# Local layers of a macaron block: order of the slot work on SyncE, TensorE and VectorE, banks of the recurrent norms, and another way to make two bias offsets

## The reference, cut to what matters

```python
x = x + 0.5 * _L0_ffn_ref(_layernorm(x), ...)      # token-mixing feed-forward
x = x + _L0_attn_ref(_layernorm(x), ...)           # 16 heads of 64, full attention with a relative bias
x = x + 0.5 * _L0_ffn_ref(_layernorm(x), ...)
x = x + 0.5 * _L1_ffn_ref(x, ...)                  # two "local" layers
x = x + _L1_attn_ref(x, ...)                       # gated recurrence over the 512 tokens
x = x + 0.5 * _L1_ffn_ref(x, ...)                  # the same two local layers again
```

```python
h = shift_token(x)                      # the second half of the features comes from the token before
q, k, v = split(h @ wqkv)               # 8 heads of 64; q and k normalised, scaled, rotated
x = x + local_attention(q, k, v) @ wo   # windows of 64 tokens, each sees itself and the one before
h = (shift_token(x) - mean) / sqrt(var + 1e-5) * lg + lb
a, g = split(h @ w1 + b1)               # 341 columns each, padded to 384
x = x + (a * gelu(g)) @ w2 + b2
```

## Time and profile before

| what | value |
|---|---|
| three runs | 1172.5, 1173.42, 1178.5 us, median 1173.42 |
| the profiled execution, its own time | 1176.82 us |
| its span, first to last instruction | 1175.0 us |
| TensorE busy | 1133.3 us, 96% of the span |
| VectorE, ScalarE, GpSimd busy | 913.7, 920.0, 617.8 us |
| mean granted TensorE clock | 0.993 of full speed |

### The profile page before, as it was taken

How to read it: one execution, slowest core, us unless ns; L and a number is a source line. 1 busy time by engine, 2 the same in 40 slices (tenths; PEclk the granted TensorE clock), 3 DMA queues, 4 the chain that set the end, 5 groups by cost and what they waited for, 6 DMA issues and landing times.

```text
span 1175.0 us, 40447 instructions
## 1 busy us (share of the span) xinstructions
PE 1133.3 (96%) x16054; PEld 728.5 (62%) x16054; DVE 913.7 (78%) x2423; ACT 920.0 (78%) x2451; POOL 617.8 (53%) x406
## 2 busy tenths in 40 slices
PE   8899999999999998999999999988999899999997
PEld 3367777677777653666666666554556566666664
DVE  5788989898989878877777777757787777777763
ACT  6877878787878777887787787876778778978874
POOL 4456666666666644664555455433454554644540
PEclk9999999999999999999999999999999999999999
DMA  8411111111111123111111111011010111111110
GB/s 291 149 39 40 58 40 57 40 57 40 57 39 57 40 85 102 42 33 42 28 42 42 22 39 33 19 33 37 15 41 20 41 32 29 44 40 28 33 42 19
DMA packets 30364, 58.36 MB, mean 50 GB/s; under 512 B 5680, under 2 KB 7152, under 8 KB 30176
## 3 DMA queue, kind: packets, MB, share of 16 engines
q1 hardware_dynamic: 30176, 55.77, 17.4%
HBM read 15.32 MB, written 1.11 MB: 14 GB/s over the span
## 4 chain that ended last, share of the span: by engine, by line
PE 83%; ACT 8%; issue 3%; DVE 3%; DMA 1%; POOL 1%; SPq 1%; ACTq 0%; POOLq 0%; DVEq 0%
PE ps L326 11%; PE ps L301 11%; PE ps L1470 6%; PE ps L1433 5%; PE ps L1400 5%; PE ps L1370 4%; PE ps L1338 4%; PE ps L1348 4%; PE ps L1440 4%; PE ps L1412 4%; PE ps L1339 4%; PE ps L1476 3%; PE ps L337 3%; PE ps L267 2%; PE ps L275 2%
## 5 line engine op out<-in xcount | busy, mean ns | idle before, releaser
L241 POOL TENSOR_TENSOR arena<-arena 128x1024 f32<-128x1024 f32 x128 | 241.0, 1893 | 147.1 <-DVE arena L536 147.0
L1280 POOL TENSOR_TENSOR arena<-arena 128x1024 f32<-128x1024 f32 x64 | 121.4, 1896 | 233.0 <-DVE arena L1856 233.0
L432 ACT ACTIVATE arena<-arena 128x512 f32<-128x512 f32 x256 | 182.4, 713 | 73.8 <-DVE arena L522 73.4
L1678 ACT ACTIVATE arena<-arena 128x128 f32<-128x128 f32 x512 | 198.3, 390 | 30.9 <-DVE arena L1848 30.3
L522 DVE CUSTOM_DVE_ANT_0 arena<-ps,arena 128x512 f32<-128x512 f32 x256 | 164.3, 688 | 26.0 <-PE ps L301 23.2
L1848 DVE CUSTOM_DVE_ANT_0 arena<-ps,near,arena 128x128 f32<-128x128 f32 x512 | 144.6, 347 | 35.2 <-PE ps L1400 35.1
L532 DVE STREAM_TRANSPOSE arena<-arena 128x1024 f32<-128x1024 f32 x128 | 157.8, 1234 | 1.1 <-POOL arena L241 0.9
L1287 POOL TENSOR_TENSOR arena<-arena 128x1024 f32<-128x1024 f32 x64 | 151.0, 2360 | 0.1
L326 PEld LDWEIGHTS ps<-arena 32*64 32x64 f32 x8192 | 118.9, 130 | 37.7 <-issue 37.3
L301 PE MATMUL ps<-arena 64*128 64x256 f32 (+1 forms) x736 | 139.9, 490 | 2.0 <-DVE arena L522 1.4
L326 PE MATMUL ps<-arena 32*64 32x128 f32 x8192 | 134.8, 274 | 1.0 <-issue 1.0
(11 more groups left out here) (161 smaller groups left out, 2196.7 us busy)
## 6 DMA issues: line engine op xcount, KB each, us to landing
arena<-arena SPq DMA_DIRECT2D x127, 128.0 KB, 2.3
arena<-arena SPq DMA_DIRECT2D x64, 192.0 KB, 2.5
arena<-rel_rows SPq DMA_DIRECT2D x16, 448.0 KB, 8.6
arena<-arena SPq DMA_DIRECT2D x64, 64.0 KB, 2.1
arena<-y SPq DMA_DIRECT2D x30, 128.0 KB, 2.3
arena<-arena SPq DMA_DIRECT2D x15, 127.8 KB, 2.3
arena<-in_wqkv SPq DMA_DIRECT2D x2, 768.0 KB, 4.8
x<-in_x SPq DMA_DIRECT2D x4, 256.0 KB, 5.0
```

Of the source, the lines that this page charges most:

```text
L241: nc.gpsimd.tensor_tensor(e, e, scale, ALU.mult).then_inc(self.normed, 1)
L432: nc.scalar.activation(self.e[:, r % 3, i, :], self.neg[:, i, :], ACT.Exp, bias=self.nmax[:, i:i + 1], scale=-1.0, accum_out=self.sums[:, ...
L1280: nc.gpsimd.tensor_tensor(e, e, self.rsum.unsqueeze(2).to_broadcast([P, H8, P]), ALU.mult).then_inc(self.p_normed, 1)
L1678: nc.scalar.activation(self.e[:, s, h, :], self.neg[:, h, :], ACT.Exp, bias=self.nmax[:, h:h + 1], scale=-1.0, accum_out=self.sums[:, s, h ...
```

## The change

It has these parts.

1. **SyncE**: `shift_z` of a group is issued ahead of `copy_halves` in the same slot, not behind it.
2. **TensorE, ups slots**: `project_v` ahead of `turn_qk`; and `weigh` after the second gate product, not after the third.
3. **TensorE, down slots**: `down` ahead of `turn_qk`.
4. **The offsets**: 12 products of one column each become 4 products with a one-column stationary operand and 384 moving columns, which leave rows; VectorE copies them to SBUF, and three transposes in the next slot turn them into columns.
5. **The recurrence's `split`**: ScalarE copies both projections out of PSUM (`copy_projected`, one copy more per sequence); VectorE splits from SBUF, in the next slot after `rotate_cos`, not at the end of its own slot from PSUM.
6. **Banks of the recurrent norms**: `middle` and `after` centre in PT's second bank and vary in the first, and each half of the next transposes waits only for its own bank; `after` of b = 0 goes to QK, where no tile is projected in the following slot, and its `scale` comes after all eight masks.
7. **b = 3**: `add_state` ahead of the second four masks, `after.centre` ahead of `turn_qk`, and on ScalarE its square ahead of `copy_qk` and its `invert` ahead of `copy_v`.
8. **Tail**: `t_vary(1)` ahead of the gate products; `copy_out` ahead of `t_square(0)`.

```diff
@@ LocalWeights
+            for a in range(2):
+                at = P // 4 * (2 * l + a)
+                last = nc.tensor.matmul(k.ps[at:at + 1, LA_O, P:P + HIDP], k.vcol(C_LNB + l), self.w1[:, l, a, :], start=True, stop=True)
         last.then_inc(self.offset_made, 1)
+
+    def turn_offsets(self, pe):
+        k, nc = self.k, self.k.nc
+        pe.wait_ge(self.offset_copied, 1)
+        for j in range(HB):
+            last = nc.tensor.transpose(k.ps[:, LA_O, (j + 1) * P:(j + 2) * P], self.offset_rows[:, j * P:(j + 1) * P], k.ident)
+        last.then_inc(self.offset_turned, 1)
@@ SlotGru
+        self.middle = SlotNorm(k, "gru_middle", LA_PT + 1, LA_PT, own_sq, own_rstd, lambda b: self.state, lambda b: self.normed,
                                lambda b: (self.scanned, b + 1), gain=k.vcol(C_GAMMA), eps=4 * LN_EPS)
+        self.after = SlotNorm(k, "gru_after", LA_PT + 1, LA_PT, own_sq, own_rstd, x, y, lambda b: (self.done, b + 1), first=(LA_QK, LA_QK + 1), last=(LA_S, LA_S + 1))
...
+        for j, to in enumerate((self.z, self.low)):
+            act.wait_ge(self.projected, 2 * b + j + 1)
+            self.k.nc.scalar.activation(to, self.k.ps[:, LA_PT + j, :], ACT.Copy).then_inc(self.copied, 1)
...
+        dve.wait_ge(self.copied, 2 * b + 2)
+        nc.vector.tensor_scalar(self.pos, self.low, k.vcol(C_BHP), 0.5, ALU.add, ALU.max).then_inc(self.split_made, 1)
+        dve.wait_ge(self.split_made, 2 * b + 1)
+        nc.vector.tensor_scalar(self.low, self.low, k.vcol(C_BH), 0.0, ALU.add, ALU.min).then_inc(self.split_made, 1)
@@ pe, one slot
-            if after is not None:
-                turn_qk(after)
             if inside:
                 wait_scores_read(slot)
                 self.gru.after.centre(pe, final)
-            if downs is not None:
+            early_v = ahead is not None and not ends and downs is None and (ups is not None)
+            if early_v:
+                project_v(ahead)
+            early_down = downs is not None and (True)
+            if early_down:
                 down(downs)
-            elif ahead is not None and not ends:
+            if after is not None:
+                turn_qk(after)
...
@@ dve, one slot
+            if final_ends == 0:
+                self.gru.after.scale(dve, final_ends)
...
             if ahead is not None:
                 rotate_cos(ahead)
+            if split is not None:
+                self.gru.split(dve, split)
```

More of the change, by code:

```diff
@@ L1261, in sp @@
                 shift(DEPTH * B + gru)
+            if norm is not None:
+                shift_z(norm)
             if ahead is not None:
                 copy_halves(ahead)
-            if norm is not None:
-                shift_z(norm)
             if down is not None and down // B in (0, DEPTH):
@@ L1449, in wait_turned_read, with wait_projected_read @@
             pe.wait_ge(self.pt_second, self.last_to(slot - 1) + 1)
+        def wait_projected_read(slot):
+            made = self.last_to(slot + 2) + 1
+            pe.wait_ge(self.squared, made)
+            pe.wait_ge(self.cos_made, made)
+            pe.wait_ge(self.sin_made, made)
         def centre(g, slot):
@@ L1514, in pe @@
                 w.offsets(pe)
+            if early == NT:
+                w.turn_offsets(pe)
             if norm is not None:
@@ L1523, in pe @@
                 self.gru.after.centre(pe, final)
-            if downs is not None:
-                down(downs)
-            elif ahead is not None and not ends:
+            early_v = ahead is not None and not ends and downs is None and (ups is not None)
[3 more added lines that the diff above has]
+            if early_down:
+                down(downs)
+            if after is not None:
+                turn_qk(after)
+            if early_down:
+                pass
+            elif downs is not None:
+                down(downs)
+            elif ahead is not None and not ends and not early_v:
                 project_v(ahead)
@@ L1530, in pe @@
             if ups is not None:
-                for c in range(HB):
-                    up(ups, slot, c, 1)
-            if last is not None:
+                up(ups, slot, 0, 1)
+                up(ups, slot, 1, 1)
                 weigh(last)
-            if downs is not None and ahead is not None:
-                project_v(ahead)
-            if ups is not None:
-                for c in range(HB):
-                    up(ups, slot, c, 0)
+                up(ups, slot, 2, 1)
+                up(ups, slot, 0, 0)
+                up(ups, slot, 1, 0)
+                up(ups, slot, 2, 0)
+            else:
+                if last is not None:
+                    weigh(last)
+                if downs is not None and ahead is not None:
+                    project_v(ahead)
             if project is not None:
@@ L1612, in pe @@
         t_centre(1)
+        t_vary(1)
         for c in range(HB):
             t_up_gate(0, c)
-        t_vary(1)
         for c in range(HB):
@@ L1754, in act @@
                 self.gru.before.invert(act, first)
+            if final == B - 1:
+                self.gru.after.square(act, final)
             if after is not None:
@@ L1757, in act @@
             if final == B - 1:
-                self.gru.after.square(act, final)
+                self.gru.after.invert(act, final)
             if ahead is not None:
                 copy_v(ahead)
-            if final == B - 1:
-                self.gru.after.invert(act, final)
             if ups is not None:
@@ L1930, in dve @@
             middle_ends, final_ends = self.gru_in(slot - 1, 4), self.gru_in(slot - 1, 5)
+            split = self.gru_in(slot - 1, 2)
             if n is not None:
@@ L1935, in dve @@
                 self.gru.middle.scale(dve, middle_ends)
-            if final_ends is not None and final_ends < B - 1:
+            if middle_ends is not None and middle_ends == B - 1:
+                self.gru.add_state(dve, middle_ends)
+            if final_ends is not None and 0 < final_ends < B - 1:
                 self.gru.after.scale(dve, final_ends)
@@ L1940, in dve @@
                     mask(n, h)
-            if middle_ends is not None:
+            if final_ends == 0:
+                self.gru.after.scale(dve, final_ends)
+            if middle_ends is not None and not (middle_ends == B - 1):
                 self.gru.add_state(dve, middle_ends)
@@ L1976, in dve @@
                     gate(ups, c)
-            if project is not None:
-                self.gru.split(dve, project)
         centred = self.t_banks(LA_QK, LA_PT)
```

85 lines of the change are left out of this document (47 added, 38 removed).

## The result

| | before | after |
|---|---|---|
| median (lowest to highest), 5 runs each | 1175.42 us (1172.5 to 1178.5) | 1157.04 us (1156.04 to 1159.59) |
| profiled execution, span | 1176.82, 1175.0 us | 1156.04, 1154.2 us |

The ratio is 0.9848, with an interval of 0.983 to 0.9866: 15.8 to 20.0 us faster. The medians differ by 18.4 us. The forecast was 1156 us, from a sum of 17.7 us.

A forecast was written before the change was run, and what follows sets the result against it. TensorE was taken as the bound, busy 1133.3 of 1175.0 us, so only standstill or slow running could be saved. Terms 3.7 + 2.8 + 1.2 + 7.4 + 2.6 = 17.7 us off 1173.4 gave 1156 us; range 1151.5 to 1163.

The forecast's parts named there:

- shift_z first: Norm slots: four waits of `centre` for a DMA go or shrink, and the clock stays up in slot 63; 3.7 us.
- Ups and down slots: Outside the recurrence: the value or down product covers `turn_qk`'s wait for `copy_turned`; 20 x 0.14 = 2.8 us.
- The rival through gelu: Ups slots: `turn_qk` behind `project_v` pushes ScalarE's chain to gelu, making the kernel slower, 1179 us; chance 0.02.
- Offsets: Offset products: clock loss recovered, less 0.35 us for the new products (some 2.6 us) and transposes; 1.2 us saved.
- The 1.55 us of clock: Behind the offset products: time lost to a granted clock of 0.50, all taken as coming back.
- Recurrence: Parts 5 to 7 and reordered slots within the recurrence: waits for masks, copies and `scale` shrink; sum 7.4 us.
- Slots 27 and 35: Recurrence: `turn_qk`'s waits go, since the split no longer keeps VectorE from the masks; 2.0 us.
- slots 29 and 30: Recurrence, `after` of b = 0 in QK's banks: slot 30 gives some 2.1 us, slot 29 0.5; 2.6 us.
- Slots 28, 36, 40 and 41: Down and ups slots of the recurrence: each gives 0.14 us, together 0.55 us.
- the wait of 1.09 for `scale` and what follows moves up by about 0.95 us: Slot 42: `centre` one step earlier lets ScalarE invert before `copy_v`; about 0.95 us gained.
- Tail: Behind the last scores: `copy_out` and `t_vary(1)` first remove waits around the gate products; 1.1 + 1.5 = 2.6 us.
- The rival "the clock stays low": Behind offsets, slots 63 or 30: each costs 1.1 to 1.6 us, all give 1160; chance 0.22, shared with returning stalls.

The follow-up runs named there:

- the second profile: The changed kernel measured and profiled once more, unaltered (5 runs): 1158.0 us, ratio to before 0.9864.
- the second profile of before: The kernel before run and profiled once more, unaltered (one run): 1176.19 us.
- the run with one row: The changed kernel with all four offset products written to partition 0 (6 runs): 1160.8 us, ratio to before 0.9888.
- parts 5 to 7 alone: The kernel before with only split from SBUF, the recurrent norms' banks and b = 3 changed (12 runs): ratio to before 0.9957.

## Why the prediction was right, and where it wasn't

The time, 1157.04 us against 1156, and most of the mechanisms were right. That it came so close is in part luck: the terms add up to 20.1 us by the second profile and not to 17.7, with errors in both directions, while the medians differ by 18.4, and two single profiles need not differ by what the medians do.

- **shift_z first** (3.7, measured 4.68). The waits for a DMA went and nothing took their place but the masks in slot 63, as said; the standstill was 1.46 us against 1.4, and the clock stayed up. The three others gave 2.93 us, not 2.1, because I summed listed waits. The list also left out short ones: six other norm slots gave 0.56 us more. TensorE at the first of them, before and after (`turn`, `centre`, `project_out`):

```profile
635.13 1.04 PE L1412 MATMUL ps<-consts,arena 128*128 128x128 f32 x8
637.02 1.13 PE L1454 MATMUL ps<-arena,consts 128*128 128x512 f32 x2 [0.86 <-DMA arena<-arena]
637.99 1.05 PE L1440 MATMUL ps<-arena 128*128 128x128 f32 x8
```
```profile
629.27 1.04 PE L1437 MATMUL ps<-consts,arena 128*128 128x128 f32 x8
630.14 1.02 PE L1485 MATMUL ps<-arena,consts 128*128 128x512 f32 x2
631.00 1.05 PE L1465 MATMUL ps<-arena 128*128 128x128 f32 x8
```

  From `turn` to `centre` it takes 1.89 us before and 0.87 after, 1.02 for a wait listed as 0.86, since without a stop the next product starts ahead of the end shown for the one in front. And behind a stop `centre` takes 0.97 to the next start, not 0.86. So this wait was worth its listed length and 0.27 us more; the same for all three would make 2.9. The term is in part one of chance: in the second profile of before the four places differ by 0.60 us in sum.
- **Ups and down slots** (2.8, measured 2.7 in 19 steps of 0.14 or 0.15 us each, and 0.37 in slot 44). The other 0.56 us of the table's 3.27 are part 1's. The rival through gelu did not occur; neither the value gates of ups slots nor `score` in down slots wait, and `weigh` waits for `add_out` once, 0.4 us in slot 31, as said.
- **Offsets** (1.2, measured 2.5). The mis-sized term is the duration of the new products: I took the spacing of 384-column products from the earlier trace rows and got 2.6 us; to four partition groups they took 0.8, which the run with one row confirms. The 1.55 us of clock came back as taken. But that the narrow products always bring the clock down is wrong. It fell behind them in five of six profiles; with parts 5 to 7 alone, which leave them as they were, TensorE shows full speed there:

```profile
502.97 2.74 PE L943 MATMUL ps<-vec,arena 128*128 128x1 f32 x24
505.57 1.07 PE L1381 MATMUL ps<-consts,arena 128*128 128x128 f32 x8
506.48 1.02 PE L1358 MATMUL ps<-arena 128*128 128x512 f32 x2
```

  The drop comes in most executions, not in all.
- **Recurrence** (7.4, measured 5.0 and 6.6, of which 0.37 is slot 44). Slots 27 and 35 gave 2.12 (said 2.0), slot 39 1.22 (1.2), slots 29 and 30 2.78 (2.6), slot 42 0.92 (0.95), and the masks of slot 27 start 1.17 us behind the scores (said 1.2). Of slot 30's 2.24 us, 1.42 were the clock drop that the second profile of before doesn't have; the move of the banks itself gives 0.8. At tile 32 0.38 us came instead of -0.2 + 0.35 = 0.15. The three instructions of the split took 0.48, 0.49 and 0.75 us, in all 1.7 as said. Slots 28, 36, 40 and 41 gave -0.09, -0.09, 0.14 and -0.09 us, in sum -0.1 and not 0.55, by the wait for L1951 that I had not seen. The step that failed is "the wait of 1.09 for `scale` and what follows moves up by about 0.95 us". What follows doesn't move up: the next copy of `shift_direct` can't end before `rotate_add` does. I followed `scale` to the scores and not to the second thing that hangs on it, though a wait of 0.79 us for it stood in the trace of before, and took VectorE's durations as its own. The price is 1.0 us of wait, and 1.7 more where the clock falls behind it. I had asked "where a stall goes" for every wait of TensorE that I removed, but not for this one.
- **Tail** (2.6, measured 3.1). The six gate products run in one piece, 2.87 us:

```profile
1143.01 0.49 PE L1627 MATMUL ps<-arena,consts 128*128 128x128 f32 x2 [0.85 <-ACT arena L1833]
1143.50 2.87 PE L1635 MATMUL ps<-arena 128*128 128x384 f32 x12
```

  The 1.07 us ahead of `project_out` are gone entirely, which I had counted, and the rest gave 2.0 instead of 1.5.
- **The rival "the clock stays low"** came at none of its places: behind the offsets and in slots 30 and 63 the products run at full speed, in all seven profiles of kernels with the whole change or nearly so. One clock loss came in slot 43, where no case of mine had it.

What stays open: why the clock falls behind the same wait (1.78, 1.88 or 2.28 us) in one execution and not in the next, why slot 44 gives 0.37 us, and where the runs of the changed kernel that weren't profiled lose it.

## What to carry to other kernels

Before you trust a loss of a microsecond in one profile, look at a second profile of the same kernel: clock drops and waits for a DMA come and go, waits for an engine stay to 0.1 us. When an operation of VectorE is moved, look at what GpSimd does at its new place, not only at what waits for it; here a copy of 0.42 us became one of 1.76, and a wait on GpSimd's side that cost nothing gave it back. And two edits that cover the same wait give it once.

## What the runs showed of the hardware

- A copy from SBUF to SBUF on VectorE (64 x 512 float32) takes 0.42 us alone. Beside an operation of GpSimd it ends 0.28 us behind that one (22 copies of 22), here up to 1.76 us in all. ScalarE's copy of the same took 0.63 us beside the same operation.
- Four float32 products with one stationary column and 384 moving ones took 0.83 us to rows in four partition groups and 2.74 us to one.
- The mean granted clock was 0.57 from 911 to 915 us, in slot 43, behind a wait of 1.78 us in one profile, and 1.00 behind the same wait in another. Behind a wait of 2.28 us it fell in three profiles of six.
